# Local attention on one core: four heads to a group in place of two, and a new order of the work between the groups

## The reference, cut to what matters

```python
h = shift_token(x)
q, k, v = jnp.split(h @ wqkv, 3, axis=-1)
q = l2norm(q) * qs
k = l2norm(k) * ksc
q, k = rotary_xpos(q, k)
...
o = local_attention(q, k, v)
...
x = x + o @ wo
```

## Time and profile before

| | |
|---|---|
| median of 3 runs | 3331.79 us (3331.76 to 3333.33) |
| profiled execution, its own time | 3330.96 us |
| span of its profile | 3328.8 us |
| TensorE busy, share of the span | 97% |
| VectorE, ScalarE, GpSimd busy | 51%, 43%, 27% |
| granted TensorE clock, mean | 0.983 |

### The profile page before, as it was taken

How to read it: one execution, slowest core, us unless ns; L and a number is a source line. 1 busy time by engine, 2 the same in 40 slices (tenths; PEclk the granted TensorE clock), 3 DMA queues, 4 the chain that set the end, 5 groups by cost and what they waited for, 6 DMA issues and landing times.

```text
span 3328.8 us, 53196 instructions
## 1 busy us (share of the span) xinstructions
PE 3227.6 (97%) x19606; PEld 2632.1 (79%) x19606; DVE 1706.7 (51%) x3549; ACT 1441.4 (43%) x2942; POOL 909.0 (27%) x1542
## 2 busy tenths in 40 slices
PE   9999999999996999999999999999995999999999
PEld 8987888888875888888877888888884888788887
DVE  4655666666665333333324666666665433334332
ACT  2116777777772111111113777777774111111111
POOL 0315544544436000000034444544444300000000
PEclk8999999999997999999999999999997999999999
DMA  4421111111114111001131111111113211111110
GB/s 149 149 68 35 53 65 61 58 61 58 55 55 114 39 38 38 13 26 39 38 116 40 61 58 61 58 58 36 61 52 97 72 51 45 51 51 51 51 38 20
DMA packets 149794, 194.82 MB, mean 59 GB/s; under 512 B 23286, under 2 KB 90998, under 8 KB 149284
## 3 DMA queue, kind: packets, MB, share of 16 engines
q1 hardware_dynamic: 133700, 175.69, 16.2%
q10 hardware_dynamic: 15840, 15.73, 1.4%
HBM read 120.06 MB, written 41.95 MB: 49 GB/s over the span
## 4 chain that ended last, share of the span: by engine, by line
PE 95%; DVE 2%; issue 1%; ACT 1%; POOL 1%; DVEq 0%; SPq 0%; POOLq 0%; ACTq 0%
PE bank L334 30%; PE bank L336 27%; PE bank L335 27%; PE bank L756 5%; PE bank L569 3%; PE bank L831 1%; DVE a_PT_lo L1309 0%; ACT a_PT_hi L1029 0%; PE bank L577 0%; ACT a_P L1024 0%; PE bank L594 0%; DVE f_hraw L1422 0%; DVE f_h L1414 0%; DVE f_rs L1409 0%; ACT f_hT_hi L1102 0%
## 5 line engine op out<-in xcount | busy, mean ns | idle before, releaser
L334 PE MATMUL bank<-f_hT_hi,f_w_hi 128*128 128x512 f32 (+1 forms) x1408 | 556.3, 395 | 15.0 <-ACT f_hT_hi L1102 13.7
L1121 ACT ACTIVATE f_gate<-bank,f_b 128x512 f32<-128x512 f32 (+1 forms) x176 | 121.1, 688 | 998.8 <-PE bank L336 998.7
L336 PE MATMUL bank<-f_hT_hi,f_w_lo 128*128 128x512 f32 (+1 forms) x1408 | 552.9, 393 | 0.0
L335 PE MATMUL bank<-f_hT_lo,f_w_hi 128*128 128x512 f32 (+1 forms) x1408 | 552.2, 392 | 0.0
L1450 DVE SCALAR_TENSOR_TENSOR f_uraw<-bank,f_b,f_gate 128x512 f32<-128x512 f32 (+1 forms) x176 | 132.1, 751 | 753.0 <-ACT f_gate L1121 752.8
L1024 ACT ACTIVATE a_P<-a_S,a_bias 128x384 f32<-128x384 f32 x512 | 310.9, 608 | 253.0 <-DVE a_bias L1299 252.9
L1299 DVE CUSTOM_DVE_ANT_0 a_S<-bank,a_masks,a_q 128x384 f32<-128x384 f32 x512 | 295.0, 614 | 64.0 <-issue 47.6
L334 PEld LDWEIGHTS bank<-f_hT_hi,f_w_hi 128*128 128x128 f32 (+1 forms) x1408 | 260.9, 185 | 77.2 <-ACT f_hT_hi L1102 14.3
L334 PE MATMUL bank<-a_PT_hi,a_V_hi 128*64 128x128 f32 x1536 | 301.1, 231 | 16.3 <-DVE a_PT_lo L1309 16.3
L336 PEld LDWEIGHTS bank<-f_hT_hi,f_w_lo 128*128 128x128 f32 (+1 forms) x1408 | 260.6, 185 | 64.3
L335 PEld LDWEIGHTS bank<-f_hT_lo,f_w_hi 128*128 128x128 f32 (+1 forms) x1408 | 261.0, 185 | 62.6
(11 more groups left out here) (167 smaller groups left out, 6883.2 us busy)
## 6 DMA issues: line engine op xcount, KB each, us to landing
a_h<-x_layer_in SPq DMA_DIRECT2D x128, 128.0 KB, 2.3
a_res<-x_layer_in SPq DMA_DIRECT2D x64, 256.0 KB, 2.9
x_after_attention<-out_tiles SPq DMA_DIRECT2D x64, 256.0 KB, 2.0
f_res<-x_after_attention SPq DMA_DIRECT2D x64, 256.0 KB, 3.3
f_stage<-in_L_ffn_w SPq DMA_DIRECT2D x60, 256.0 KB, 3.4
f_h<-x_after_attention ACTq DMA_DIRECT2D x28, 512.0 KB, 4.3
c_x<-in_x SPq DMA_DIRECT2D x32, 256.0 KB, 3.1
x_layer_in<-out_tiles SPq DMA_DIRECT2D x32, 256.0 KB, 2.0
```

Source lines behind the costliest of these rows:

```text
L334: pe.matmul(dst, w[0], m[0], start=start, stop=False)
L335: pe.matmul(dst, w[0], m[1], start=False, stop=False)
L336: return pe.matmul(dst, w[1], m[0], start=False, stop=stop)
L1121: act.activation(f_gate[0:ROWS[m], m % 2, :], bank[pair_of(u, m, end) + 1][0:ROWS[m], :], ACT.Gelu, bias=f_b1[0:ROWS[m], 1, m:m + 1]).then ...
```

## The change

The loop has two half tiles of four heads (g = 0, 1) for the scores and for P times V: `scores(x, g)` makes two pairs, head by head in turn within each pass, in banks 0 to 3; `pv(x, g)` makes four heads, 36 products, in one bank. Transposes of P stay in pairs, but `a_PT` holds four heads. q's and h's transposes go into bank 5 and k's into bank 6, the two banks of the P transposes, and `q_project` and `project_out` use bank 0 (`spare`). The bodies of TensorE, ScalarE and VectorE are written in a new order. On TensorE `k_T`, `h_T` and `k_project` stand between `pv(t, 0)` and `scores(t + 1, 0)`; `p_T(t, 3)` is the last piece of a step, and `pv(t, 1)` the first of the next. ScalarE's and VectorE's `p_T(t, 3)` are their last pieces as well.

```diff
+        GROUPS = PAIRS // 2
+        work, spare, o_bank, q_turn, k_turn = bank[7], bank[0], bank[4], bank[5], bank[6]
+        h_turn = lambda x: bank[6] if x < 2 else bank[5]
+        q_work = lambda x: work if x == 0 else spare
         SPLIT_BY_ACT = 3
         FHTS = BLOCKS * KT_
...
-                    pe.wait_ge(a_k_copied, START + G + x + 1)
-                    pe.wait_ge(a_k_squared, START + G + x + 1)
-                    project(0, x, a_q_mm)
+                    if x == 0:
+                        pe.wait_ge(a_k_copied, START + G + 1)
+                        pe.wait_ge(a_k_squared, START + G + 1)
+                    else:
+                        pe.wait_ge(a_S_masked, START + (G + x - 1) * H + 1)
+                    project(0, x, q_work(x), a_q_mm)
 
...
                 def project_out(x):
-                    pe.wait_ge(a_O_hi, START + 2 * (G + x + 1))
-                    pe.wait_ge(a_O_lo, START + 2 * (G + x + 1))
-                    if here(x + 2):
-                        pe.wait_ge(a_V_lo, START + G + x + 3)
-                    elif x > 0:
-                        pe.wait_ge(a_out_set, START + G + x)
+                    pe.wait_ge(a_O_hi, START + 2 * GROUPS * (G + x + 1))
+                    pe.wait_ge(a_O_lo, START + 2 * GROUPS * (G + x + 1))
+                    if here(x + 1):
+                        pe.wait_ge(a_S_masked, START + (G + x + 1) * H + H // 2 + 1)
                     if x == 0:
                         pe.wait_ge(a_w_lo, START + 4 * l + 4)
                     for k in range(PAIRS):
-                        mm = three_passes(pe, work[:], [a_OT[i][:, k, :] for i in range(2)],
+                        mm = three_passes(pe, spare[:], [a_OT[i][:, k, :] for i in range(2)],
                                           [a_w[3][i][:, k, :] for i in range(2)], k == 0, k == PAIRS - 1)
                     mm.then_inc(a_wo_mm, 1)
 
-                def scores(x, i):
+                def scores(x, g):
                     j = x % QUAD
-                    if i == 0:
+                    if g == 0:
                         if x == 0:
                             pe.wait_ge(a_carry_zero, START + 4 * l + 4)
                             if l == 0:
@@ -741,35 +745,50 @@
                             pe.wait_ge(a_carried, START + (l * (BLOCKS - 1) + x // QUAD) * 64)
                         for ready in (a_QT_hi, a_QT_lo, a_KT_hi, a_KT_lo):
                             pe.wait_ge(ready, START + G + x + 1)
-                    pe.wait_ge(a_S_masked, START + (G + x) * H + 2 * i)
-                    for odd in range(2):
-                        r = slice(odd * HD, odd * HD + HD)
-                        three_passes(pe, bank[odd][:, 0:WIN * P], [a_QT[n][r, x % 2, i, :] for n in range(2)],
-                                     [a_KT[n][r, i, j * P:(j + WIN) * P] for n in range(2)], True, True)\
-                            .then_inc(a_S_mm, 1)
+                        if x >= 2:
+                            pe.wait_ge(a_out_set, START + G + x - 1)
+                    elif here(x + 1):
+                        pe.wait_ge(a_q_copied, START + G + x + 2)
+                        pe.wait_ge(a_q_squared, START + G + x + 2)
+                    pe.wait_ge(a_S_masked, START + (G + x) * H + g * H // 2)
+                    for i in (2 * g, 2 * g + 1):
+                        for step, (q_part, k_part) in enumerate(((0, 0), (0, 1), (1, 0))):
+                            for odd in range(2):
+                                r = slice(odd * HD, odd * HD + HD)
+                                mm = pe.matmul(bank[2 * (i % 2) + odd][:, 0:WIN * P], a_QT[q_part][r, x % 2, i, :],
+                                               a_KT[k_part][r, i, j * P:(j + WIN) * P], start=(step == 0), stop=(step == 2))
+                                if step == 2:
+                                    mm.then_inc(a_S_mm, 1)
 
                 def p_T(x, i):
                     pe.wait_ge(a_P_set, START + (G + x) * H + 2 * i + 2)
                     pe.wait_ge(a_PT_lo, START + (G + x) * PAIRS + i)
+                    if i == 0 and here(x + 2):
+                        pe.wait_ge(a_hT_lo, START + G + x + 3)
+                    if i == 2 and here(x + 3):
+                        pe.wait_ge(a_hT_lo, START + G + x + 4)
+                    if i == 2 and here(x + 1):
+                        pe.wait_ge(a_QT_lo, START + G + x + 2)
+                        pe.wait_ge(a_KT_lo, START + G + x + 2)
                     for odd in range(2):
                         for kb in range(WIN):
                             mm = pe.transpose(pt_banks[:, odd, kb * P:(kb + 1) * P],
                                               a_P[:, (2 * i + odd) % 4, kb * P:(kb + 1) * P], ident[:])
                     mm.then_inc(a_PT_mm, 1)
 
-                def pv(x, i):
-                    if i == 0:
+                def pv(x, g):
+                    if g == 0:
                         pe.wait_ge(a_V_hi, START + G + x + 1)
                         pe.wait_ge(a_V_lo, START + G + x + 1)
-                        pe.wait_ge(a_O_lo, START + (G + x) * 2)
-                    pe.wait_ge(a_PT_hi, START + (G + x) * PAIRS + i + 1)
-                    pe.wait_ge(a_PT_lo, START + (G + x) * PAIRS + i + 1)
-                    for odd in range(2):
-                        h = 2 * i + odd
+                    pe.wait_ge(a_O_lo, START + 2 * (GROUPS * (G + x) + g))
+                    pe.wait_ge(a_PT_hi, START + (G + x) * PAIRS + 2 * g + 2)
+                    pe.wait_ge(a_PT_lo, START + (G + x) * PAIRS + 2 * g + 2)
+                    for h in range(4):
+                        head = 4 * g + h
                         for kb in range(WIN):
-                            mm = three_passes(pe, bank[4 + odd][0:HD, i * P:(i + 1) * P],
-                                              [a_V[n][:, x % QUAD + kb, h * HD:(h + 1) * HD] for n in range(2)],
-                                              [a_PT[n][:, odd, kb * P:(kb + 1) * P] for n in range(2)],
+                            mm = three_passes(pe, o_bank[0:HD, h * P:(h + 1) * P],
+                                              [a_V[n][:, x % QUAD + kb, head * HD:(head + 1) * HD] for n in range(2)],
+                                              [a_PT[n][:, h, kb * P:(kb + 1) * P] for n in range(2)],
                                               kb == 0, kb == WIN - 1)
                     mm.then_inc(a_PV_mm, 1)
...
                 def body():
                     for t in STEPS:
+                        if here(t - 1):
+                            pv(t - 1, 1)
                         if here(t):
                             scores(t, 1)
-                        if here(t - 1):
-                            pv(t - 1, 3)
-                        if here(t):
                             p_T(t, 0)
                         if here(t + 1):
                             v_project(t + 1)
-
                         if here(t):
-                            scores(t, 2)
-                            pv(t, 0)
                             p_T(t, 1)
+                        if here(t - 1):
+                            project_out(t - 1)
                         if here(t + 1):
                             q_T(t + 1)
-                        if here(t - 1):
-                            project_out(t - 1)
 
                         if here(t):
-                            scores(t, 3)
-                            pv(t, 1)
-                            p_T(t, 2)
+                            pv(t, 0)
                         if here(t + 1):
                             k_T(t + 1)
+                        if here(t + 3):
+                            h_T(t + 3)
                         if here(t + 2):
                             k_project(t + 2)
-
                         if here(t + 1):
                             scores(t + 1, 0)
                         if here(t):
-                            pv(t, 2)
-                            p_T(t, 3)
-                        if here(t + 3):
-                            h_T(t + 3)
+                            p_T(t, 2)
                         if here(t + 2):
                             q_project(t + 2)
+                        if here(t):
+                            p_T(t, 3)
 
...
                 def body():
                     for t in STEPS:
-                        if here(t + 1) and t >= 0:
-                            square(0, t + 1)
-                            q_copy(t + 1)
                         if here(t):
                             exp(t, 2)
+                            exp(t, 3)
                         if here(t - 1):
-                            o_hi(t - 1)
+                            o_hi(t - 1, 1)
                         if here(t):
                             p_T(t, 0)
-                            exp(t, 3)
                             normalize(t, 1)
+                            exp(t, 4)
+                            exp(t, 5)
                         if here(t + 1):
```

(84 more changed lines are left out.)

96 lines of the change are left out of this document (49 added, 47 removed).

## The result

| | before | after |
|---|---|---|
| median | 3332.01 us (4 runs, 3331.76 to 3333.33) | 3515.55 us (4 runs, 3515.21 to 3516.93) |
| span of the profile | 3328.8 us | 3513.6 us |
| granted TensorE clock, mean | 0.983 | 0.963 |

The changed kernel is slower by 5.5%: ratio 1.0551, 95% interval 1.0532 to 1.0569. The forecast was 3545 us with a range of 3450 to 3610; the excess over before was 184 us where 214 were forecast.

The account below looks back on a forecast made before the run. TensorE's own row of instructions was taken to bound attention. Spacing -37, wait +171, `q_project` +6, clock +66 and layer ends +8 made +214 us: span 3328.8 + 214 = 3543, median 3545 us, range 3450 to 3610.

Parts of the forecast that it names:

- The wait before `pv(t, 1)`: TensorE stands after `p_T(t, 3)` until ScalarE copies and VectorE subtracts: 2.85 us per tile, +171 us.
- Nothing else waits but `q_project`: In steady tiles, the only other new TensorE wait is `q_project`'s, for head 0's mask: 0.1 us per tile, +6 us.
- The spacing: Fewer changes between kinds of product on TensorE save 0.61 us per tile, bounds 0.5 to 0.75: -37 us.
- The clock: TensorE's granted clock falls with the new wait, costing 1.1 us per tile, bounds 0 to 1.7: +66 us.
- The ends of the layers: In the last two tiles, seven or eight TensorE waits where six were: +4 us per layer, +8 us.
- The order of the heads: Alternating heads in `scores` costed at nothing; as rival, saves 1.4 us per tile, 3459 us, chance 0.03.
- the clock's staying up: Rival: the wait is there, but work around it holds TensorE's clock up: 3479 us, chance 0.20.
- a longer ScalarE chain: Rival: longer ScalarE chain or second wait in `p_T(t+1, 1)`, another 0.5 + 0.6 us per tile: 3611 us, chance 0.11.
- the faster case: Rival: `pv(t, 1)` finds its input nearly ready and the clock stays: 3295 us, chance 0.05.

Follow-up runs that it names:

- e1: The changed kernel, but heads 6 and 7's products read the P of heads 4 and 5, cutting the wait (a test, output differs): 3277.9 us, ratio 0.9844.
- e3: The changed kernel with ten unread products of 512 columns between the last P transposes and the products of P and V: 3456.5 us, ratio 1.0381.
- e6: The changed kernel with `normalize(t + 1, 0)` moved behind square, `q_copy` and the last P copy on ScalarE: 3481.7 us, ratio 1.0453.
- e2: The changed kernel with a pair's scores issued as before, three passes of one head, then three of the other: 3515.2 us, ratio 1.0555.
- e4: The changed kernel with `scores(t, 1)` moved ahead of `pv(t - 1, 1)` on TensorE: 3415.2 us, ratio 1.0257.
- e7: The changed kernel with `pv(t, 1)` split: products of heads 4 and 5, then `scores(t + 1, 1)`, then heads 6 and 7: 3344.4 us, ratio 1.0045.
- e9: e7 plus `normalize(t + 1, 0)` behind ScalarE's last P copy and masks of heads 4 and 5 ahead of `o_lo` on VectorE: 3282.7 us, ratio 0.9855.
- e5: The changed kernel with the last P transposes ahead of `q_project` on TensorE, and their ScalarE and VectorE work moved earlier: 3434.8 us, ratio 1.0311.

## Why the prediction was right, point by point

- **The wait before `pv(t, 1)`:** forecast 2.85 us per tile, measured 2.8 (2.86 less 0.06 at that place; and 25.1 - 22.3 between the tiles of after and of e1), 2.62 as the timeline counts idle time. e1 shows that it is the cause, e3 that its length does not depend on what TensorE does meanwhile, e6 that 0.3 of it is ScalarE's queue (forecast 0.35).
- **Nothing else waits but `q_project`:** right. Forecast 0.1, measured 0.13.
- **The spacing:** right in sign, mis-sized. Forecast -0.61 us per tile, bounds 0.5 to 0.75; measured 22.3 - 0.13 - 23.07 = -0.90 (e1). The steady tiles of before and e1, added up from start to start by kind, show where the other 0.3 lies. The scores gave 0.40, as forecast (0.38). The P transposes are what the sum had wrong: it added 0.10 for their new place behind the scores, and they gave 0.22 (without `q_project`'s wait). Before, three of the four blocks had a further block of transposes behind them and took 0.68; the sum knew only the fourth, which takes 0.60. After, none has, and they take 0.58 to 0.63. The projections gave 0.42 where my rows made 0.27. The other way went 0.12 in the products of P and V, whose first one behind transposes holds up the next for 0.14 where I had at most 0.11, and 0.06 in the transposes of q, k and h. The first pair of lines is before, the second e1.

```profile
...
700.57 0.84 PE L756 MATMUL bank<-ident,a_P 128*128 128x128 f32 x6
701.25 0.60 PE L569 MATMUL bank<-ident,a_h 128*128 128x128 f32 x4
...
```

```profile
...
607.69 0.82 PE L775 MATMUL bank<-ident,a_P 128*128 128x128 f32 x6
608.27 0.47 PE L338 MATMUL bank<-a_wo_hi,a_OT_hi 128*128 128x512 f32 x1
...
```

- **The clock:** forecast 1.1 us per tile, bounds 0 to 1.7; measured 25.96 - 25.10 = 0.86. A fall costs 1.5 us (26.6 - 25.1), and 16 of 27 tiles have one. So the term is of the right size, but its picture was not: I had spread a loss of 1.1 over every wait, and there are tiles with a whole loss and tiles with none. That 1.1 came from waits at the ends of the layers, and no row told how many of the new waits would bring a fall; that the term came within 0.24 us is in part luck.
- **The ends of the layers:** forecast seven or eight waits for six, and +8 us. The list has seven at layer 0's end. With 60 x 2.89 = 173 us for the steady tiles, 11 of the 185 us of span are left for ends and starts, a remainder that was not taken apart further.
- **The order of the heads:** costed at nothing; e2 measures -0.4 us, nothing.

The sum with the measured terms: 60 x (2.80 + 0.13 - 0.90 + 0.86) = 173, and 11 for the ends: the 184.8 us by which the span grew. The forecast of +214 was 30 too high: 17 from the spacing and 14 from the clock, with 3 from the wait; `q_project` and the ends were 5 too low. The two large misses point the same way, so the forecast does not owe its place in the range to their cancelling.

Of the rivals, the clock's staying up came true in 11 of 27 tiles; in every tile it did so only with shorter waits than this one (e4, e7); a longer ScalarE chain didn't come; the faster case exists only with the link cut or covered (e1, e9), and then at 3278 to 3283 us, below the 3295 that I gave for it.

## What to carry to other kernels

Before you merge small groups to save changes between kinds of matmul, count the covers: each block whose result must pass through other engines needs a piece of independent work behind it, as long as that chain (here a wait of 2.15 us in e5 to 2.8 us in the change, for a copy and a subtraction). When one is missing, look for a piece that is ready and cut it in two, as the four heads' products here: half of them together with the scores covered all but 0.3 us (e7), where the scores alone left 0.4 us there and opened a wait of 0.8 us before themselves (e4). Then walk the other engines' queues: two moves in them were worth 62 us, 1.8% (e7 to e9).

## What the runs showed of the hardware that I had not expected

- How often the clock fell went with the length of the wait that comes once per tile: after 2.8 us in 16 of 27 tiles, after 2.5 in 12 of 27, after 2.15 in 6 of 28, and in none with waits of about 1 us or with the wait filled. Each fall to 1.2 GHz cost 1.5 to 1.6 us. The length of the wait does not decide it alone: in the changed kernel the step into `pv` is 3.42 to 3.46 us in tiles with a fall and 3.34 to 3.46 in tiles without one, and the two kinds of tile take turns; and the wait of 2.15 us stands at another place than the others (e5). What decides is not shown. Ten products whose result nobody reads won back 59 us.
- A block of six transposes takes 0.58 to 0.60 us before a projection and 0.68 before another block of transposes (steady tiles, before and e1).
- Products on the two halves of the array's rows ran side by side even when the program had three of one half before three of the other, with no cost in time (3515.2 against 3515.6 us).
